# Macaron block on one core: attention runs all heads of batch 0, then all of batch 1

## The chip, the cores and the metric

One core of a Trainium2 chip runs the whole program. Its engines have queues of their own and wait for each other on semaphores: PE (TensorE, matrix multiply), DVE (VectorE), ACT (ScalarE), POOL (GpSimd) and SP (SyncE, which here only issues DMAs). The metric is device microseconds of the slowest core. The kernel before has a median of 596.48 us in three runs (592.13 to 601.65).

## The reference

A macaron block over x of 2 x 512 tokens, 256 wide: half a mixture of experts, attention, half a mixture of experts again, each on a layer-normed x and added to it.

```
x = x + 0.5 * ffn(layernorm(x))
x = x + attention(layernorm(x))
x = x + 0.5 * ffn(layernorm(x))

# attention: B, S, D = 2, 512, 256;  H, HKV, DH = 16, 4, 128;  four query heads share one key/value head
q = rope(x @ wq.T); k = rope(x @ wk.T); v = x @ wv.T
# causal, linear (no softmax); each head h has its own decay lam[h], the same for both batches
o[i] = sum over j <= i of (q[i] . k[j]) * exp(-lam[h] * (i - j)) * v[j]
return o.reshape(b, s, H * DH) @ wo.T
```

The two batches do not meet in attention: what they share are the weights and the decays. The experts' layers (32 experts of 96, 16 small ones of 128, four per token) are not touched.

## The kernel before

The program runs expert layer, attention, expert layer. Attention works in **units**: one head of one batch, 512 tokens. There are 32 (`UNITS`), and unit n is head n // 2 of batch n % 2 (`B` = 2). Four heads share a key/value head, so eight units (`GU`) use one group g; keys and values of group g + 1 are made while group g runs.

Five kinds of work carry a letter in the code. `("q", n, b)` is the query projection of unit n, `("k", g, b)` the key projection, `("v", g, b)` the value projection, `("t", g, b)` the transposition of the first 256 keys, and in the splits `("o", h)` stands for the output weights. `projections(n, place)` says which of them unit n runs: in place "scores" the query projection of unit n + 1, in place "behind" one piece for the next group (v, v, k, k, t, t in units 2 to 7 of a group). The lists `order` and `split_order` are the orders in which all engines go through projections and splits, and positions in them are the values that semaphores wait for.

**Splits.** Query, key and output projections run as three products of high and low parts in place of one. So each weight of 128 x 256 is split in two: ACT copies the high part (`split_hi`, L555) and POOL subtracts it from the whole for the low part (`split_lo`, L448), which raises `w_split`. PE waits for `w_split` before a projection or an output. A split of a query or output weight serves both batches of a head here: 16 + 16, and 4 for keys. `splits(n)` says which splits unit n makes: output weights when n is even, query weights of head (n + 3) // 2 when n is odd, which PE wants in unit n + 2.

**One unit on PE**, in order (L1252 to L1265): scores of the first half (L1193) and the chunk state (L1199), query projection of the next unit (L1180, six matmuls of 512 columns), scores of the second half (L1193), output projection of the unit before (L1231, twelve matmuls), the piece "behind" (L1180, L1171 or L1165), then the products with the values (L1217, L1214).

**Beside it.** DVE subtracts for the low half of the output (L941), applies the decay mask (L932), copies the state (L934), rotates the new query from PSUM (L920 to L922), masks the second half and rotates a key. POOL goes through its unit as follows: add the two parts of the rotated query (L526, raises `roped`, which the next scores wait for), multiply its second half by the decays (L533), make the splits of the unit (L448), add a rotated key if there is one (L526). ACT scales values (L579), makes the high parts (L555), copies projected values and keys (L570), and copies the output from PSUM (L690). All projections but the first five write bank 0 of PSUM, so each waits until the one before it has been read.

**Loads.** SP issues per head: wq after the projection of two heads earlier, decays after `pv_mm`, wo after `wo_mm` (`load_head`, L409), each into one of two buffers, and wk and wv once per group.

**Start and end.** Before unit 0 PE runs q, k, v, v, k, t (`projections(-1, None)`). At the end ACT copies the sums of x and attention out of four PSUM banks (`residual_out`, L672): batch 0's four tiles once output 30 is done, batch 1's after output 31.

## Time and profile before

| | |
|---|---|
| median of three runs | 596.48 us (592.13 to 601.65) |
| profiled execution | 596.83 us, span 595.1 us, mean granted clock 0.929 |
| PE busy | 507.6 us, 85% of the span |
| PE weight load (PEld) busy | 439.8 us, 74% |
| DVE busy | 318.7 us, 54% |
| POOL busy | 257.4 us, 43% |
| ACT busy | 142.8 us, 24% |
| costliest group | L1180, projections from split weights: x240, 65.2 us, 407 ns each |
| chain that ended last | PE 60%, DVE 22%, DMA 11%, issue 3% |

The profile describes one execution. "Busy" leaves out the waits; a line's idle time is what its engine spent before it, with the operation that ended most of it. An average over the span mixes three stages, so what a change in attention is worth must be read from a stretch of attention alone: with start times from the timeline, and busy times from windows.

### The profile page before, as it was taken

Reading aid. Unit: us, or ns where it says so; the run is one execution under the profiler, and the core shown is the slowest. Engines: PE = TensorE matmul, PEld = TensorE weight load, DVE = VectorE, ACT = ScalarE, POOL = GpSimd, SP = SyncE. Lnnn points to the kernel's source line nnn. Section 1 sums busy time; section 2 is a strip of 40 time slices with the busy share of each in tenths; the row PEclk is TensorE's granted clock in tenths of the full one; section 3 lists DMA queues with packets and bytes.
Section 4 is the critical chain, followed back from the end, with each engine's and each line's share of the span. In section 5 each row is a group of like instructions: output and inputs, shape, how many; then the busy total and the mean of one; then the engine's idle time right before and its main releaser. Section 6 shows DMA issues by size and latency. Waiting matters only on the chain.

```text
span 595.1 us, 9863 instructions
## 1 busy us (share of the span) xinstructions
PE 507.6 (85%) x3276; PEld 439.8 (74%) x3276; DVE 318.7 (54%) x997; ACT 142.8 (24%) x382; POOL 257.4 (43%) x280
## 2 busy tenths in 40 slices
PE   8589979999039999999999999999858999999900
PEld 7489968887017888889888988888758898888600
DVE  6844333343296647664766476666785444444325
ACT  4102212222234231222132212211420222222211
POOL 0045656663236444434443444333103566666322
PEclk9789999999559999999999999999976999999955
DMA  7989987781650010121012011110295425778173
GB/s 228 322 261 330 331 319 245 257 287 55 236 192 18 28 36 19 54 56 23 31 40 68 19 36 36 52 37 10 86 381 179 154 94 182 234 251 281 55 256 118
DMA packets 46654, 87.79 MB, mean 148 GB/s; under 512 B 6528, under 2 KB 27264, under 8 KB 46592
## 3 DMA queue, kind: packets, MB, share of 16 engines
q1 hardware_dynamic: 37376, 66.05, 34.0%
q0 software_dynamic: 6912, 18.88, 9.4%
q10 hardware_dynamic: 2304, 2.10, 1.0%
q8 instruction: 31, 0.51, 0.4%
q14 instruction: 31, 0.25, 0.1%
HBM read 74.42 MB, written 12.58 MB: 146 GB/s over the span
## 4 chain that ended last, share of the span: by engine, by line
PE 60%; DVE 22%; DMA 11%; issue 3%; SPq 2%; ACT 1%; POOL 1%; POOLq 0%; DVEq 0%; ACTq 0%
PE bank L1180 10%; PE bank L1089 8%; PE bank L1084 7%; PE bank L1217 6%; DMA w_down_sb<-w_down 4%; PE bank L1108 4%; PE bank L1110 4%; PE bank L1193 4%; DVE shared L921 3%; DVE shared L922 3%; DVE shared L920 3%; DMA shared<-z_dram 3%; PE bank L1214 3%; PE bank L1171 3%; PE bank L1199 2%
## 5 line engine op out<-in xcount | busy, mean ns | idle before, releaser
L458 POOL DMA_INDIRECT decay_all<-xn_dram,ids x72 | 69.6, 966 | 121.0 <-PE bank L1056 52.8
L526 POOL TENSOR_TENSOR shared<-shared 128x512 f32<-128x512 f32 x36 | 45.8, 1273 | 130.2 <-DVE shared L922 130.2
L860 DVE COPY oT_all<-bank 128x256 f32<-128x256 f32 x72 | 30.6, 425 | 131.0 <-PE bank L1056 131.0
L467 POOL DMA_INDIRECT z_dram<-probs_all,dest x72 | 70.2, 975 | 36.4 <-ACT probs_all L642 32.7
L1180 PE MATMUL bank<-split_sb 128*128 128x512 f32 x240 | 65.2, 407 | 1.9 <-ACT split_sb L601 0.9
L1089 PE MATMUL bank<-w_ch_sb,oT_all 128*128 128x256 f32 x256 | 65.7, 379 | 0.0
L941 DVE TENSOR_TENSOR split_sb<-bank,split_sb 128x512 fp32r<-128x512 f32 x32 | 22.1, 692 | 66.2 <-ACT split_sb L690 66.2
L634 ACT ACTIVATE rot<-bank 128x224 f32<-128x224 f32 x72 | 25.7, 357 | 132.2 <-PE bank L1089 132.2
L1084 PE MATMUL bank<-w_exp_sb,oT_all 128*128 128x192 f32 x256 | 53.4, 331 | 2.9 <-issue 1.6
L1231 PE MATMUL bank<-split_sb 128*128 128x256 f32 x384 | 53.4, 288 | 1.5 <-DVE split_sb L941 1.5
L1084 PEld LDWEIGHTS bank<-w_exp_sb,oT_all 128*128 128x128 f32 x256 | 43.8, 189 | 10.3 <-issue 5.5
L1180 PEld LDWEIGHTS bank<-split_sb 128*128 128x128 f32 x240 | 42.2, 189 | 10.7 <-DVE shared L922 1.9
L1089 PEld LDWEIGHTS bank<-w_ch_sb,oT_all 128*128 128x128 f32 x256 | 46.9, 190 | 3.3
L1231 PEld LDWEIGHTS bank<-split_sb 128*128 128x128 f32 x384 | 47.8, 190 | 1.7 <-issue 1.7
L690 ACT ACTIVATE split_sb<-bank 128x512 fp32r<-128x512 f32 x32 | 19.1, 597 | 118.5 <-PE bank L1217 118.5
L642 ACT ACTIVATE probs_all<-bank 128x256 f32<-128x256 f32 x72 | 27.6, 383 | 69.2 <-PE bank L1110 69.2
L920 DVE TENSOR_TENSOR shared<-bank,rot 128x512 f32<-128x512 f32 x40 | 27.7, 691 | 25.7 <-PE bank L1180 25.7
L932 DVE TENSOR_TENSOR probs_all<-bank,decay_all 128x256 f32<-128x256 f32 (+1 forms) x128 | 39.5, 350 | 1.0
L1108 PE MATMUL bank<-w_down_sb,wkv_sb 96*128 96x256 f32 x128 | 38.2, 380 | 0.0
L1110 PE MATMUL bank<-w_ch_sb,wkv_sb 128*128 128x256 f32 x128 | 38.2, 379 | 0.0
L1006 PE MATMUL bank<-ident_sb,xn_sb 128*128 128x128 f32 x48 | 11.3, 325 | 26.2 <-DVE xn_sb L762 25.8
L905 DVE SCALAR_TENSOR_TENSOR x_sb<-shared,wgt,x_sb 128x256 f32<-128x256 f32 x36 | 17.8, 524 | 27.1 <-POOL x_sb L501 27.0
(141 smaller groups left out, 971.3 us busy)
## 6 DMA issues: line engine op xcount, KB each, us to landing
shared<-w_up_piece SPq DMA_DIRECT2D x32, 448.0 KB, 6.3
w_exp_sb<-w_exp SPq DMA_DIRECT2D x32, 384.0 KB, 8.3
shared<-w_down_piece SPq DMA_DIRECT2D x32, 256.0 KB, 4.3
w_ch_sb<-w_ch SPq DMA_DIRECT2D x16, 384.0 KB, 5.9
shared<-z_dram SPq DMA_DIRECT2D x12, 512.0 KB, 7.1
decay_all<-decay SPq DMA_DIRECT2D x16, 256.0 KB, 2.7
w_down_sb<-w_down SPq DMA_DIRECT2D x16, 192.0 KB, 7.8
xn_dram<-xn_sb ACTq DMA_DIRECT2D x16, 128.0 KB, 6.1
```

Source lines behind the costliest of these rows:

```text
L458: pool.indirect_dma_start(out=xg[s], out_offset=None, in_=xn_dram[l][:, :], in_offset=bass.IndirectOffsetOnAxis(ap=ids[:, SEQ[t]:SEQ[t] + ...
L467: pool.indirect_dma_start(out=z_dram[l][:, :], out_offset=bass.IndirectOffsetOnAxis(ap=dest[:, SEQ[t]:SEQ[t] + 1], axis=0), in_=y_sb[s], i ...
L526: nc.gpsimd.tensor_tensor(dst, rope_a[r % 2], rope_b[r % 2], ALU.add).then_inc(roped, 1)
L920: nc.vector.tensor_tensor(rope_a[r % 2], ps[:, :], cos_sb, ALU.mult)
L932: ins = nc.vector.tensor_tensor(probs[c][:, a:b], sc_ps[c][:, a:b], decay_sb[h % 2][:, 0:b - a], ALU.mult)
L1084: nc.tensor.matmul(h2[rows, :, 0:MI], xgT[s][:, k, rows], up_e[:, k * 2 * MI:(k + 1) * 2 * MI].rearrange("p (a n) -> p a n", a=2), start=( ...
L1089: ins = nc.tensor.matmul(h2[rows, :, MI:WI], xgT[s][:, k, rows], up_c[:, k * 2 * CI:(k + 1) * 2 * CI].rearrange("p (a n) -> p a n", a=2), ...
L1108: nc.tensor.matmul(y_ps[s][rows, 0:D], actT[s][0:MI, 0, rows], down_e, start=True, stop=False)
L1110: ins = nc.tensor.matmul(y_ps[s][rows, 0:D], actT[s][:, 1, rows], down_c, start=False, stop=True)
L1180: ins = nc.tensor.matmul(proj_bank[at][:, :], w[:, k, :], x[:, k, b * S:(b + 1) * S], start=(k == 0 and w is hi and x is xnT_hi), stop=(k ...
L1217: ins = nc.tensor.matmul(o_ps[:, j * P:(c + 1) * HALF], v_sb[g % 2][:, b * SB + j, :], probs[c][:, t * HALF:t * HALF + HALF - t * P], star ...
L1231: ins = nc.tensor.matmul(res_ps[(n % B) * SB + t], o[n % 2][:, cols], w, start=False, stop=False, skip_group_check=True)
```

## The change

Unit n becomes head n % 16 of batch n // 16: all heads of batch 0, then all heads of batch 1. A key/value group G now means one group of one batch. It serves four units, there are eight of them (`GS`), and each brings one k, one v and one t, in places m = 1, 2, 3 of the four units of the group before. Key and value buffers are halved accordingly, and no longer lie in `xn_sb`. Since neighbouring units have different heads, every unit loads and splits weights of its own: 32 loads each of wq, wo and decays where there were 16, 8 of wk and wv where there were 4, and 72 splits on ACT and on POOL where there were 36. The split of q is made two units ahead of its unit (`("q", n + 2)` in `splits(n)`), and stands behind that of o. Each unit has its own weights, so the loads are issued piecewise (`load_q`, `load_o`, `load_decay`). Before unit 0 stand q, k, v, t in place of q, k, v, v, k, t, and a third split. The copies of batch 0's four tiles wait for output 15 in place of output 30; their place in ACT's program stays. The indices in ACT's, DVE's and POOL's helpers follow the new units, and are left out of the diff below.

```diff
--- before.py
+++ after.py
@@ -146,11 +146,9 @@
...
         kqT = shared[:, 0:4 * S].rearrange("p (a s) -> p a s", s=S)
         v_all = sb("v_all", [P, TT * DH])
 
-        xn_flat = xn_sb[:, :, :].rearrange("p t d -> p (t d)")
-        kT = [[kqT[:, b, :] for b in range(B)], [xn_flat[:, b * S:(b + 1) * S] for b in range(B)]]
+        kT = [kqT[:, u, :] for u in range(2)]
         qT = [kqT[:, 2 + u, :] for u in range(2)]
-        v_sb = [v_all[:, :].rearrange("p (t d) -> p t d", t=TT),
-                xn_flat[:, B * S:2 * B * S].rearrange("p (t d) -> p t d", t=TT)]
+        v_sb = [v_all[:, u * S:(u + 1) * S].rearrange("p (t d) -> p t d", t=SB) for u in range(2)]
...
@@ -287,35 +284,32 @@
 
 
 
-        UNITS, GU = H * B, GROUPS * B
+        UNITS, GS = H * B, HKV * B
+
 
         def projections(n, place):
 
-
-            g, m = n // GU, n % GU
+            G, m = n // GROUPS, n % GROUPS
             if n < 0:
-                return [("q", 0, 0), ("k", 0, 0), ("v", 0, 0), ("v", 0, 1), ("k", 0, 1), ("t", 0, 0)]
+                return [("q", 0), ("k", 0), ("v", 0), ("t", 0)]
             if place == "scores":
-                return [("q", n + 1, (n + 1) % B)] if n + 1 < UNITS else []
-            if g + 1 < HKV and m >= 2:
-                return [("vvkktt"[m - 2], g + 1, m % 2)]
-            return [("t", 0, 1)] if n == 0 else []
+                return [("q", n + 1)] if n + 1 < UNITS else []
+            return [("vkt"[m - 1], G + 1)] if m >= 1 and G + 1 < GS else []
 
         def splits(n):
 
             if n < 0:
-                return [("q", 0), ("k", 0)]
-            found = [("o", n // 2)] if n % 2 == 0 else [("q", (n + 3) // 2)] if n + 3 < UNITS else []
-            if n == 0:
-                found.append(("q", 1))
-            if n % GU == 3 and n // GU + 1 < HKV:
-                found.append(("k", n // GU + 1))
+                return [("q", 0), ("k", 0), ("q", 1)]
+            found = [("o", n)]
+            if n + 2 < UNITS:
+                found.append(("q", n + 2))
+            if n % GROUPS == 1 and n // GROUPS + 1 < GS:
+                found.append(("k", n // GROUPS + 1))
             return found
 
         def split_buffer(key):
             kind, n = key
             return (kind, 0 if kind == "k" else n % 2)
-
 
         split_order = [key for n in range(-1, UNITS) for key in splits(n)]
         order = projections(-1, None)
@@ -324,7 +318,7 @@
         rotated = [p for p in order if p[0] in "qk"]
         copied = [p for p in order if p[0] in "vt"]
 
-        proj_bank = [bank[a] for a in (2, 3, 6, 0, 1)] + [bank[0]] * (len(order) - 5)
+        proj_bank = [bank[a] for a in (2, 3, 6, 1)] + [bank[0]] * (len(order) - 4)
 
         block = ctx.enter_context(nc.Block())
 
@@ -399,36 +393,50 @@
 
             stage_quads(sp, 0)
 
-            def load_kv(g):
-                if g >= 1:
-
-                    sp.wait_ge(proj_mm, max(order.index((kind, g - 1, 1)) for kind in "kv") + 1)
-                sp.dma_start(wk_sb, wk[g, :, :]).then_inc(kv_in, 16)
-                sp.dma_start(wv_sb, wv[g, :, :]).then_inc(kv_in, 16)
-
-            def load_head(h):
-                u = h % 2
-                if h >= 2:
-                    sp.wait_ge(proj_mm, order.index(("q", 2 * (h - 2) + 1, 1)) + 1)
-                sp.dma_start(wq_sb[u], wq[h, :, :]).then_inc(wq_in[u], 16)
-                if h >= 2:
-                    sp.wait_ge(pv_mm, B * (h - 1))
-                sp.dma_start(decay_sb[u], decay[h, :, :]).then_inc(decay_in[u], 16)
-                if h >= 2:
-                    sp.wait_ge(wo_mm, 2 * (h - 1))
-                sp.dma_start(wo_sb[u], wo[h, :, :]).then_inc(wo_in[u], 16)
+            def load_kv(G):
+                if G >= 1:
+                    sp.wait_ge(proj_mm, max(order.index((kind, G - 1)) for kind in "kv") + 1)
+                sp.dma_start(wk_sb, wk[G % HKV, :, :]).then_inc(kv_in, 16)
+                sp.dma_start(wv_sb, wv[G % HKV, :, :]).then_inc(kv_in, 16)
+
+            def load_q(n):
+                if n >= 2:
+                    sp.wait_ge(proj_mm, order.index(("q", n - 2)) + 1)
+                sp.dma_start(wq_sb[n % 2], wq[n % H, :, :]).then_inc(wq_in[n % 2], 16)
+
+            def load_decay(n):
+                if n >= 2:
+                    sp.wait_ge(masked[1], n - 1)
+                    sp.wait_ge(q_scaled, n - 1)
+                sp.dma_start(decay_sb[n % 2], decay[n % H, :, :]).then_inc(decay_in[n % 2], 16)
+
+            def load_o(n):
+                if n >= 2:
+                    sp.wait_ge(wo_mm, n - 1)
+                sp.dma_start(wo_sb[n % 2], wo[n % H, :, :]).then_inc(wo_in[n % 2], 16)
 
             def first_loads():
                 load_kv(0)
-                load_head(0)
+                load_q(0)
+                load_q(1)
+                load_decay(0)
                 sp.dma_start(cos_sb, cos[:, :]).then_inc(const_in, 16)
                 sp.dma_start(sin_sb, sin[:, :]).then_inc(const_in, 16)
 
             load_results(sp, 0, first_loads)
-            for h in range(1, H):
-                load_head(h)
-                if h % GROUPS == 1 and h // GROUPS + 1 < HKV:
-                    load_kv(h // GROUPS + 1)
+            load_o(0)
+            load_decay(1)
+            load_q(2)
+            load_kv(1)
+            for n in range(UNITS):
+                if n + 3 < UNITS:
+                    load_q(n + 3)
+                if n + 1 < UNITS:
+                    load_o(n + 1)
+                if n + 2 < UNITS:
+                    load_decay(n + 2)
+                if n % GROUPS == 3 and n // GROUPS + 2 < GS:
+                    load_kv(n // GROUPS + 2)
 
             sp.wait_ge(wo_mm, UNITS)
             for c in range(NCH):
@@ -664,13 +671,12 @@
...
         def _(act_e):
             moe_act(act_e, 0)
             norm_act(act_e, 1)
-            copy_projected(act_e, ("v", 0, 0))
+            copy_projected(act_e, ("v", 0))
             scale_values(act_e, 0)
-            copy_projected(act_e, ("v", 0, 1))
-            copy_projected(act_e, ("t", 0, 0))
+            copy_projected(act_e, ("t", 0))
 
             def residual_out(i):
-                act_e.wait_ge(wo_mm, UNITS - 1 if i < SB else UNITS)
+                act_e.wait_ge(wo_mm, H if i < SB else UNITS)
                 nc.scalar.activation(x_sb[:, i, :], res_ps[i], ACT.Copy).then_inc(x2_copied, 1)
...
@@ -1144,25 +1148,22 @@
...
-                kind, n, b = p
+                kind, n = p
+                b = n // H if kind == "q" else n // HKV
                 at = order.index(p)
-                if at == 5:
-                    pe.wait_ge(kv_copied, 2)
+                if at in (3, 4):
+                    pe.wait_ge(xnT_copied, 2 * TT)
                 elif at >= 5 and order[at - 1] in copied:
                     pe.wait_ge(kv_copied, copied.index(order[at - 1]) + 1)
                 elif at >= 5:
                     pe.wait_ge(rope_read, rotated.index(order[at - 1]) + 1)
-                else:
+                if kind != "t":
                     pe.wait_ge(xnT_copied, TT + (b + 1) * SB)
...
@@ -1214,21 +1211,20 @@
...
             def output(n):
-                h = n // B
-                key = ("o", h)
+                key = ("o", n)
                 pe.wait_ge(w_split, split_order.index(key) + 1)
                 pe.wait_ge(o_split, n + 1)
...
                 for t in range(SB):
                     cols = slice(t * P, (t + 1) * P)
                     for o, w in ((oT_hi, hi), (oT_lo, hi), (oT_hi, lo)):
-                        ins = nc.tensor.matmul(res_ps[(n % B) * SB + t], o[n % 2][:, cols], w, start=False, stop=False,
+                        ins = nc.tensor.matmul(res_ps[(n // H) * SB + t], o[n % 2][:, cols], w, start=False, stop=False,
                                                skip_group_check=True)
...
```

The first place is POOL's queue in two neighbouring units early in attention. L526 (L534 after) is the add of the rotated query, L533 (L540) its product with the decays, L448 (L456) a split: wq_all holds query weights, wo_all output weights, wkv_sb key weights. Before:

```order
L526 TENSOR_TENSOR shared<-shared 128x512
L533 TENSOR_TENSOR state_sb<-shared,decay_all 128x256
L448 TENSOR_TENSOR split_sb<-wq_all,split_sb 128x256
L526 TENSOR_TENSOR shared<-shared 128x512
L533 TENSOR_TENSOR state_sb<-shared,decay_all 128x256
L448 TENSOR_TENSOR split_sb<-wo_all,split_sb 128x256
```

After, from the same unit (unit 1, and unit 2):

```order
L534 TENSOR_TENSOR shared<-shared 128x512
L540 TENSOR_TENSOR state_sb<-shared,decay_all 128x256
L456 TENSOR_TENSOR split_sb<-wo_all,split_sb 128x256
L456 TENSOR_TENSOR split_sb<-wq_all,split_sb 128x256
L456 TENSOR_TENSOR split_sb<-wkv_sb,split_sb 128x256
L534 TENSOR_TENSOR shared<-shared 128x512
L540 TENSOR_TENSOR state_sb<-shared,decay_all 128x256
L456 TENSOR_TENSOR split_sb<-wo_all,split_sb 128x256
L456 TENSOR_TENSOR split_sb<-wq_all,split_sb 128x256
```

Each unit now has both splits, o ahead of q, where it had one of the two.

The second place is PE's queue at the start of attention: L1180 (L1181 after) are query and key projections, six rows each, L1171 (L1172) value projections, L1165 (L1166) the transposition, L1193 the first scores. Before:

```order
L1180 MATMUL bank<-split_sb 128x512 x12
L1171 MATMUL bank<-wkv_sb,shared 128x128 x16
L1180 MATMUL bank<-split_sb 128x512 x6
L1165 MATMUL bank<-ident_sb,shared 128x128 x2
L1193 MATMUL bank<-shared 128x256
```

After:

```order
L1181 MATMUL bank<-split_sb 128x512 x12
L1172 MATMUL bank<-wkv_sb,shared 128x128 x8
L1166 MATMUL bank<-ident_sb,shared 128x128 x2
L1193 MATMUL bank<-shared 128x256
L1193 MATMUL bank<-shared 128x128
```

The second value projection and the second key projection are no longer ahead of the first scores.

## Rows read from the trace of the kernel before

**Rows 1.** Windows over attention: stretch, us, busy us by engine, PEclk, DMA share.

```profile
190.80:412.21 221.41, 217.91 (x1342) 193.63 (x1340) 136.10 (x290) 51.61 (x137) 91.56 (x100) 1.00 0.13 38
```

**Rows 2.** Timeline of a plain interval: start us, length us, engine, line, operation.

```profile
392.16 1.64 PE L1180 MATMUL bank<-split_sb 128*128 128x512 f32 x6
...
393.83 0.69 DVE L920 TENSOR_TENSOR shared<-bank,rot 128x512 f32<-128x512 f32 x1 [0.45 <-PE bank L1180]
...
396.00 1.26 POOL L526 TENSOR_TENSOR shared<-shared 128x512 f32<-128x512 f32 x1 [3.93 <-DVE shared L922]
...
397.35 0.73 POOL L533 TENSOR_TENSOR state_sb<-shared,decay_all 128x256 f32<-128x256 f32 x1
...
398.02 0.60 ACT L690 ACTIVATE split_sb<-bank 128x512 fp32r<-128x512 f32 x1 [5.20 <-PE bank L1217]
...
398.03 0.73 POOL L448 TENSOR_TENSOR split_sb<-wq_all,split_sb 128x256 fp32r<-128x256 f32 x1
...
398.84 1.63 PE L1180 MATMUL bank<-split_sb 128*128 128x512 f32 x6
```

**Rows 3.** Timeline, PE: query projections that begin v, k and t intervals.

```profile
213.40 1.63 PE L1180 MATMUL bank<-split_sb 128*128 128x512 f32 x6
...
221.87 1.64 PE L1180 MATMUL bank<-split_sb 128*128 128x512 f32 x6
...
290.13 1.64 PE L1180 MATMUL bank<-split_sb 128*128 128x512 f32 x6
...
298.21 1.64 PE L1180 MATMUL bank<-split_sb 128*128 128x512 f32 x6
...
305.07 1.63 PE L1180 MATMUL bank<-split_sb 128*128 128x512 f32 x6
```

**Rows 4.** Timeline, PE and POOL: the interval with output and query split.

```profile
190.80 1.64 PE L1180 MATMUL bank<-split_sb 128*128 128x512 f32 x6
...
194.71 1.27 POOL L526 TENSOR_TENSOR shared<-shared 128x512 f32<-128x512 f32 x1 [1.58 <-DVE shared L922]
...
196.06 0.72 POOL L533 TENSOR_TENSOR state_sb<-shared,decay_all 128x256 f32<-128x256 f32 x1
...
196.74 0.73 POOL L448 TENSOR_TENSOR split_sb<-wo_all,split_sb 128x256 fp32r<-128x256 f32 x1
...
197.42 0.73 POOL L448 TENSOR_TENSOR split_sb<-wq_all,split_sb 128x256 fp32r<-128x256 f32 x1
...
198.25 1.62 PE L1180 MATMUL bank<-split_sb 128*128 128x512 f32 x6 [0.28 <-issue]
```

**Rows 5.** Timeline, PE and POOL: start of attention.

```profile
180.08 4.23 POOL L508 TENSOR_TENSOR split_sb<-shared,split_sb 128x256 fp32r<-128x256 f32 x6
...
181.68 3.01 PE L1180 MATMUL bank<-split_sb 128*128 128x512 f32 x12 [0.92 <-ACT split_sb L601]
...
184.52 3.73 PE L1171 MATMUL bank<-wkv_sb,shared 128*128 128x128 f32 x32
...
187.71 1.28 POOL L526 TENSOR_TENSOR shared<-shared 128x512 f32<-128x512 f32 x1
...
189.48 0.38 PE L1165 MATMUL bank<-ident_sb,shared 128*128 128x128 f32 x2
```

**Rows 6.** DMA issues with us to landing, and timeline of SP.

```profile
wo_all<-wo SPq DMA_DIRECT2D x5, 128.0 KB, 2.0
...
389.21 0.33 SPq L419 DMA_DIRECT2D wo_all<-wo  x1
```

**Rows 7.** Windows, columns as in the first group, around a low clock.

```profile
148.00:150.00 2.00, 0.34 (x2) 0.00 (x0) 0.00 (x0) 1.07 (x2) 1.52 (x2) 1.00 0.41 133
...
150.00:152.00 2.00, 0.00 (x0) 0.00 (x0) 0.00 (x0) 0.80 (x2) 0.40 (x1) 0.91 0.24 78
...
178.00:180.00 2.00, 1.81 (x8) 0.89 (x8) 1.83 (x9) 2.00 (x9) 1.35 (x2) 0.76 0.00 0
```

**Rows 8.** Timeline, ACT: copy of the last unit's output.

```profile
423.00 0.60 ACT L690 ACTIVATE split_sb<-bank 128x512 fp32r<-128x512 f32 x1 [0.53 <-PE bank L1217]
```

More of the change, by code:

```diff
@@ L557, in copy_projected @@
         def copy_projected(act_e, p):
-            kind, g, b = p
+            kind, G = p
             act_e.wait_ge(proj_mm, order.index(p) + 1)
@@ L941, in split_output @@
                 nc.vector.tensor_tensor(oT_lo[n % 2], o_ps[:, :], oT_hi[n % 2].bitcast(f32), ALU.subtract).then_inc(o_split, 1)
-            rotate(("q", 0, 0))
-            rotate(("k", 0, 0))
-            rotate(("k", 0, 1))
+            rotate(("q", 0))
+            rotate(("k", 0))
             for n in range(UNITS):
@@ L1154, in project @@
                     pe.wait_ge(rope_read, rotated.index(order[at - 1]) + 1)
-                else:
+                if kind != "t":
                     pe.wait_ge(xnT_copied, TT + (b + 1) * SB)
-                if kind == "q":
-                    key = ("q", n // B)
-                elif kind == "k":
-                    key = ("k", n)
                 if kind == "t":
-                    pe.wait_ge(roped, rotated.index(("k", n, b)) + 1)
+                    pe.wait_ge(roped, rotated.index(("k", n)) + 1)
                     for t in range(2):
                         cols = slice(t * P, (t + 1) * P)
-                        ins = nc.tensor.transpose(proj_bank[at][:, cols], kT[n % 2][b][:, cols], ident_sb[:])
+                        ins = nc.tensor.transpose(proj_bank[at][:, cols], kT[n % 2][:, cols], ident_sb[:])
                 elif kind == "v":
@@ L1173, in project @@
                 else:
-                    pe.wait_ge(w_split, split_order.index(key) + 1)
+                    pe.wait_ge(w_split, split_order.index(p) + 1)
                     pe.wait_ge(xnT_split, (b + 1) * SB)
                     hi, lo = [w.rearrange("p (k n) -> p k n", k=KD)
-                              for w in (w_hi[split_buffer(key)], w_lo[split_buffer(key)])]
+                              for w in (w_hi[split_buffer(p)], w_lo[split_buffer(p)])]
                     for k in range(KD):
@@ L1203, in products @@
             def products(n):
-                g, b = n // GU, n % B
+                G = n // GROUPS
                 pe.wait_ge(o_split, n)
-                if n == 0:
-                    pe.wait_ge(rope_read, rotated.index(("k", 0, 1)) + 1)
-                if n % GU < B:
-                    pe.wait_ge(kv_copied, copied.index(("v", g, b)) + 1)
+                pe.wait_ge(kv_copied, copied.index(("v", G)) + 1)
                 for c in range(2):
```

53 lines of the change are left out of this document (25 added, 28 removed).

## The prediction

> **What bounds the kernel now.** I read the page first (PE 85% busy, POOL 43%, ACT 24%), then windows to find attention, then the timeline of all engines in one unit. Attention's main stretch runs from the query projection of unit 1 (190.80) to that of unit 31 (412.21): 221.41 us, with PE busy for 217.91 of them at full clock, and POOL for 91.56 [rows 1]. So on average PE sets the pace and POOL is idle over half the time. That average is not enough here: the change puts work on POOL, and PE waits for POOL's results in a given order.
>
> I therefore measure each unit from one query projection to the next on PE, which I call an interval. A plain one takes 398.84 - 392.16 = 6.68 us [rows 2]. With a value projection behind it takes 221.87 - 213.40 = 8.47, with a key projection 298.21 - 290.13 = 8.08, with a transposition 305.07 - 298.21 = 6.86 [rows 3]. The first, which also holds two residual matmuls and a transposition, takes 198.25 - 190.80 = 7.45 [rows 4]. Before has 30 intervals: 11 plain, 6 of each kind and the first, together 73.5 + 140.5 + 7.45 = 221.4, the whole stretch. So nothing else is in it.
>
> Now POOL inside a plain interval [rows 2]. The query projection starts at 392.16, DVE begins to rotate its result at 393.83, POOL adds it at 396.00 (3.84 after the projection's start), multiplies it by the decays at 397.35 and makes its one split at 398.03, done at 398.76. The next query projection starts at 398.84, but its weights had been split a unit earlier, so it waits for none of this.
>
> **What changes in an interval.** Each unit now makes the output split and then the split of the query weights of two units on, which PE wants in the very next unit. The trace of before shows this pair once, in unit 0, where head 0's output and head 1's query weights are both split: add 194.71, multiply 196.06, split 196.74, split 197.42 to 198.15, and PE starts the projection at 198.25 [rows 4]. This is 3.54 us from the start of the add to the projection that needs its result. All of it hangs on POOL's order: the add cannot begin before the rotation, and the two splits stand behind it, though their inputs have long been there. So the loop is query projection, rotation, add, multiply, split, split, query projection, and it takes 3.84 + 3.54 = 7.38 us. An interval now lasts as long as this or as its old length, whichever is more. A plain one goes from 6.68 to 7.38 (+0.70), one with a transposition from 6.86 to 7.38 (+0.52); those with a value or key projection (8.47, 8.08) hide it, though a key split stands behind the query split in the former, since nobody waits for that one until a unit later.
>
> **How many.** After the change the 30 intervals are: places m = 1, 2, 3 of the first seven groups with v, k and t (7 each), and 9 plain (eight with m = 0, unit 0 among them, and unit 29). Unit 0 keeps its residual matmuls in place of an output projection of about the same length and loses its transposition, so I take it as plain.
> - Without any stall the new mix would take 9 x 6.68 + 7 x (8.47 + 8.08 + 6.86): against before two plain intervals and the first go, and one of each kind comes, -13.36 - 7.45 + 23.41 = **+2.6 us**. This is the value and the key projection that stood before unit 0 and now stand inside.
> - The stall adds 9 x 0.70 + 7 x 0.52 = **+9.9 us**. Its bounds: 0, should POOL's splits be done in time, and 9 x 0.75 + 7 x 0.57 = 10.7, should the splits take their full 0.73 us each in place of the 0.68 between their starts. I take the measured chain.
>
> **The start.** Before unit 0 PE loses eight value and six key matmuls, some 3.5 us of its time. That gives nothing, for the first scores need the rotated key of batch 0, and its way stays: two rotations on DVE, then POOL's add at 187.71, 1.28 long [rows 5]. Before, PE came to the transposition at 189.48, half a microsecond after that add, because of the second projections; now it will wait for the add itself. And a third split on POOL (0.7) now stands before the six subtractions from 180.08, whose second one the first projection (181.68) waits for [rows 5]. So the transposition comes at 187.71 + 0.70 + 1.28 + 0.05 = 189.74, or **+0.3 us**. Bounds: -0.4 if the third split costs nothing, +0.7 if all of it counts.
>
> **What I cost at nothing.** ACT gets 36 more high parts of 0.4 us; it idles 5.20 us ahead of each output copy (row of 398.02 in [rows 2]), and without this cover a unit would take 0.4 more. Loads: SP now issues three per unit. The wo of the next unit goes out when output n - 1 is done, as at 389.21, and lands 2.0 us later [rows 6], at 391.2; ACT comes to its split at about 392.4, once it has copied the output and scaled the values, so 1.2 us are left. Decays go out after the second mask and have over four microseconds. DVE has nothing new. The residual copies of batch 0 (1.2 us) can run earlier, but ACT stands idle 0.53 us just before it copies the last output [rows 8], so they were hidden: 0. The expert layers are as before.
>
> **Sum:** 2.6 + 9.9 + 0.3 = +12.8 us. The profiled execution took 596.83, 0.35 above the median of 596.48; I put the sum on both alike: **609.3 us** as a median, 2.1% slower. The measurement of this kernel tells about 2% from no change, or 608.4 us here.
>
> **Rivals.**
> - *POOL keeps ahead.* The condition is that the query split is done 2.84 us after the add starts, 0.70 earlier than measured in unit 0. Then only the mix and the start count: +2.9, 599.4 us, no change that could be told. For it speaks that POOL is idle more than half of the stretch, against it that its idle time lies before the add. The Trainium skill (GPSIMD Engine Reference, section 3.1) gives about 2.6 cycles per element for an operation with two inputs, at 1.2 GHz; by that a split is an estimated 0.56 us and the add 1.11, the chain would take some 2.8 us in place of 3.54, and this rival would hold. The rows stand against it: 0.73 for a split or a product and 1.27 for the add [rows 2, 4].
> - *The clock falls in the gap at the start.* With less before unit 0, PE idles from about 187.2 (the one value projection then ends) to 189.7, 2.5 us. After PE's last work of the first expert layer the clock stayed full for over 1.6 us beyond 150, where PE had done only 0.34 us in the 2 us before, and later was back only within 178 to 180 (0.76 there) [rows 7]. A fall would cost about 2 to 4 us of matmuls at half speed: near 612. The Trainium skill (TensorE: Matmul & The Clock Gate, Part 1) calls the half clock the default that only activity releases; it would allow such a fall, and the trace has none for so short a gap.
> - *A load comes late.* Should wo take over 3.2 us, ACT's split of o and with it q's would slip. It needs nearly 4 us, twice what is measured, before POOL waits too. Each microsecond of that in 30 units would be 30 us: 620 or more.
> - *Faster.* Everything taken away, 3.5 us of PE at the start and 1.2 us on ACT, stays under 12 us even if it all counted.
>
> **Numbers.** Forecast 0.81, its own range 606 to 613 with the scatter of medians (the three runs lie 0.8% to either side). POOL keeps ahead 0.09, clock 0.05, late load 0.03, something faster 0.02. The range 602 to 615 leaves out the first rival's centre and the late load. Slower by over 2% means above 608.4: three in five of the forecast (0.49), and the clock and load rivals (0.08) give 0.57; faster 0.02; within 2% 0.41.
>
> **What would show it.** In the profile after, plain intervals of 7.38 us with POOL's second split ending just before each query projection on PE, and PE idle there, released by POOL's split line; value and key intervals unchanged at 8.47 and 8.08; the transposition at about 189.7 behind POOL's add, counted from the same start; attention's stretch near 234 us. Plain intervals of 6.68 would prove the first rival, longer ones with ACT waiting for a DMA the third, a PEclk of 0.5 near 190 the second. If value or key intervals grow too, the loop is longer than I measured.

## The result, and the profile after

The changed kernel took **612.78 us** (median of four runs, 611.56 to 617.05) beside 596.32 for the kernel before (592.13 to 601.65): ratio **1.0313, 95% interval 1.023 to 1.0396**. The ratios and intervals here and below are taken over fast executions alone, so they are not the quotients of the medians. The forecast was 609.3, slower, with a range of 602 to 615. Sign and range were right; the median is 3.5 us above the forecast.

The profiled execution of the changed kernel took 611.56 us (span 609.9). First the page: busy time per engine, the chain that ended last, and the group of the query projection.

```profile
PE 515.9 (85%) x3276; PEld 444.3 (73%) x3276; DVE 320.4 (53%) x997; ACT 153.6 (25%) x418; POOL 282.5 (46%) x316
...
PE 33%; issue 22%; POOL 21%; DVE 10%; DMA 10%; SPq 2%; ACT 1%; POOLq 0%; DVEq 0%; ACTq 0%
...
L1181 PE MATMUL bank<-split_sb 128*128 128x512 f32 x240 | 65.0, 407 | 10.0 <-POOL split_sb L456 8.8
```

PE is still busy for 85% of the span, and a reader of the first line alone would call it the bound as before. The second line says otherwise: of the chain that ended last, PE holds 33% where it held 60%, and POOL 21%. The third says where: the query projection (L1180 before, L1181 now) idles 10.0 us, 8.8 of them behind POOL's split. The list of waits over attention (us in total, times, longest) counts them:

```profile
PEld bank L1181 <- issue: 11.4, 16, 0.8
PE bank L1181 <- POOL split_sb L456: 8.8, 16, 0.6
...
PE bank L1166 <- POOL shared L534: 2.7, 1, 2.7
```

Sixteen waits: nine plain intervals and seven with a transposition, the number that the prediction gave. Here is PE in four successive intervals, one of each kind (k, t, plain, v), from the timeline:

```profile
273.33 1.63 PE L1181 MATMUL bank<-split_sb 128*128 128x512 f32 x6
...
281.41 1.62 PE L1181 MATMUL bank<-split_sb 128*128 128x512 f32 x6
...
288.98 1.63 PE L1181 MATMUL bank<-split_sb 128*128 128x512 f32 x6 [0.48 <-POOL split_sb L456]
...
296.52 1.62 PE L1181 MATMUL bank<-split_sb 128*128 128x512 f32 x6 [0.62 <-POOL split_sb L456]
...
304.98 0.71 PE L1181 MATMUL bank<-split_sb 128*128 128x512 f32 x2
```

The value interval is 304.98 - 296.52 = 8.46 and the key interval 281.41 - 273.33 = 8.08, as before [rows 3]. The transposition's went from 6.86 to 288.98 - 281.41 = 7.57, the plain one from 6.68 [rows 2] to 296.52 - 288.98 = 7.54. The windows over attention, in the columns of [rows 1]; the second is from the first projection to unit 1's:

```profile
194.02:430.50 236.48, 224.49 (x1363) 197.84 (x1362) 138.10 (x293) 63.06 (x173) 114.99 (x134) 1.00 0.26 74
185.22:194.02 8.80, 6.14 (x38) 5.41 (x39) 4.14 (x6) 2.68 (x9) 5.91 (x7) 1.00 0.14 45
```

So the stretch from unit 1's query projection to unit 31's grew from 221.41 to 236.48, **+15.07 us**; PE's work in it grew by 224.49 - 217.91 = 6.6, with 12.0 us of idle time in place of 3.5. One whole loop, in the timeline of PE and POOL:

```profile
320.59 1.62 PE L1181 MATMUL bank<-split_sb 128*128 128x512 f32 x6 [0.44 <-POOL split_sb L456]
...
324.43 1.27 POOL L534 TENSOR_TENSOR shared<-shared 128x512 f32<-128x512 f32 x1 [4.09 <-DVE shared L928]
...
325.77 0.73 POOL L540 TENSOR_TENSOR state_sb<-shared,decay_all 128x256 f32<-128x256 f32 x1
...
326.46 0.73 POOL L456 TENSOR_TENSOR split_sb<-wo_all,split_sb 128x256 fp32r<-128x256 f32 x1
...
327.15 0.73 POOL L456 TENSOR_TENSOR split_sb<-wq_all,split_sb 128x256 fp32r<-128x256 f32 x1
...
328.10 0.53 PEld L1181 LDWEIGHTS bank<-split_sb 128*128 128x128 f32 x3 [0.78 <-issue]
328.13 0.70 PE L1181 MATMUL bank<-split_sb 128*128 128x512 f32 x2 [0.62 <-POOL split_sb L456]
```

This is the shape of [rows 4], now in the middle of attention. Projection to addition takes 324.43 - 320.59 = 3.84, as predicted. Addition to next projection takes 328.13 - 324.43 = 3.70 in place of 3.54. The split ends at 327.15 + 0.73 = 327.88 and PE starts 0.25 later; in [rows 4] it started 198.25 - (197.42 + 0.73) = 0.10 later.

For the start, both kernels are counted from their first row transposition of the attention part, since up to there PE's program is the same: 167.66 before, 170.52 after. That these lie 2.86 apart is scatter, for the kernels below, equal up to this point, have it between 164.77 and 168.40. Part of it can be seen: in the first expert layer the clock of the changed kernel's profile falls once more, behind a PE gap of 3.08 us (0.53 over 82 to 84 us, 0.62 over 84 to 86), where the kernel before has 1.00 behind a gap of 3.58 us.

```profile
167.66 0.69 PE L1006 MATMUL bank<-ident_sb,xn_sb 128*128 128x128 f32 x2 [19.32 <-DVE xn_sb L762]
```
```profile
170.52 0.69 PE L1010 MATMUL bank<-ident_sb,xn_sb 128*128 128x128 f32 x2 [19.82 <-DVE xn_sb L768]
...
185.22 3.01 PE L1181 MATMUL bank<-split_sb 128*128 128x512 f32 x12 [0.45 <-ACT split_sb L608]
...
192.67 0.41 PE L1166 MATMUL bank<-ident_sb,shared 128*128 128x128 f32 x2 [2.65 <-POOL shared L534]
...
194.02 1.17 PE L1181 MATMUL bank<-split_sb 128*128 128x512 f32 x4
```

From there the first projection comes after 14.70 us (before 14.02, [rows 5]), the transposition after 22.15 (before 21.82), unit 1's projection after 23.50 (before 23.14, [rows 4]): the start costs +0.36.

The two profiled times differ by 611.56 - 596.83 = 14.73: +2.86 before attention, +0.36 at the start, +15.07 in the stretch, -3.56 behind unit 31's projection. Of the last, nothing lies in attention, for output 31 follows that projection by about 12.25 us in both; all of it lies in the second expert layer, which is the same code. The first and the last number together are -0.7 and scatter; attention is what has to be explained.

### The profile page after: what moved, and what is told of

Read it like the earlier page. It is cut to its first block, busy times and chain, and to the rows that moved or that the text cites. A ratio compares the mean times of both kernels' runs of the same rounds, so it can differ in the third digit from the quotient of the medians.

```text
span 609.9 us, 10064 instructions
## 1 busy us (share of the span) xinstructions
PE 515.9 (85%) x3276; PEld 444.3 (73%) x3276; DVE 320.4 (53%) x997; ACT 153.6 (25%) x418; POOL 282.5 (46%) x316
## 4 chain that ended last, share of the span: by engine, by line
PE 33%; issue 22%; POOL 21%; DVE 10%; DMA 10%; SPq 2%; ACT 1%; POOLq 0%; DVEq 0%; ACTq 0%
PE bank L1093 8%; POOL shared L534 8%; POOL split_sb L456 8%; PE bank L1088 7%; DMA w_down_sb<-w_down 4%; PE bank L1112 4%; PE bank L1114 4%; POOL state_sb L540 4%; DVE x_sb L911 3%; PE bank L1060 2%; PE bank L1001 2%; DMA shared<-w_up_piece 2%; DMA shared<-z_dram 1%; PE bank L1102 1%; DMA probs_all<-z_dram 1%
## 5 line engine op out<-in xcount | busy, mean ns | idle before, releaser
L534 POOL TENSOR_TENSOR shared<-shared 128x512 f32<-128x512 f32 x40 | 51.0, 1276 | 125.8 <-DVE shared L928 125.7
L1181 PE MATMUL bank<-split_sb 128*128 128x512 f32 x240 | 65.0, 407 | 10.0 <-POOL split_sb L456 8.8
L1181 PEld LDWEIGHTS bank<-split_sb 128*128 128x128 f32 x240 | 42.1, 188 | 21.3 <-issue 11.4
L1193 PE MATMUL bank<-shared 128*128 128x256 f32 (+1 forms) x256 | 52.3, 327 | 0.0
L1214 PE MATMUL bank<-probs_all,v_all 128*128 128x256 f32 (+1 forms) x256 | 52.2, 326 | 0.0
L1214 PEld LDWEIGHTS bank<-probs_all,v_all 128*128 128x128 f32 x256 | 46.8, 190 | 6.1 <-issue 0.5
L1193 PEld LDWEIGHTS bank<-shared 128*128 128x128 f32 x256 | 46.0, 190 | 5.9
```

The source lines that it names most:

```text
L534: nc.gpsimd.tensor_tensor(dst, rope_a[r % 2], rope_b[r % 2], ALU.add).then_inc(roped, 1)
L1181: ins = nc.tensor.matmul(proj_bank[at][:, :], w[:, k, :], x[:, k, b * S:(b + 1) * S], start=(k == 0 and w is hi and x is xnT_hi), stop=(k ...
L1193: ins = nc.tensor.matmul(sc_ps[c][:, t * HALF:t * HALF + HALF - t * P], kT[G % 2][:, j * P:(j + 1) * P], qT[n % 2][:, j * P:(c + 1) * HALF ...
L1214: ins = nc.tensor.matmul(o_ps[:, j * P:(c + 1) * HALF], v_sb[G % 2][:, j, :], probs[c][:, t * HALF:t * HALF + HALF - t * P], start=(j == 0 ...
```

## Experiments

Theory A: attention loses its time because POOL ends the query split too late for the next projection (the loop above), plus what PE adds before it starts. The rivals: the amount of POOL's work, the order of batches itself (more work or other waits inside the stretch), the clock. Each kernel below is compared with the kernel before, run on the same chip (median 595.22 for kernels 1 to 4, 596.57 for 5 to 8, 595.54 for 9). The recorded expectations use labels: e1 to e4 are kernels 1 to 4, e7 is kernel 5, e5 kernel 6, e6 kernel 7, e9 kernel 8 and e8 kernel 9; q1 and q31 are the query projections of units 1 and 31.

**1. Query split ahead of the output split.** The changed kernel, with the two splits of a unit swapped.

```diff
-            found = [("o", n)]
-            if n + 2 < UNITS:
-                found.append(("q", n + 2))
+            found = [("q", n + 2)] if n + 2 < UNITS else []
+            found.append(("o", n))
```

> The changed kernel, with the query split ahead of the output split in each unit, on ACT and POOL. Same work, same number of splits. Theory (PE waits for a chain on POOL: add, multiply, split o, split q): the chain gets one split shorter, 7.54 - 0.68 = 6.86 us, so plain intervals take 6.86 and those with a transposition stay at their old 6.86; 9 x 0.68 + 7 x 0.68 = 10.9 us less than after: near 602, stretch from q1 to q31 near 225.6. Rival (POOL has too much to do in all, or the added loads and high parts cost the time): no change, 612.8.

Measured: **602.64 us** (600.81 to 603.79), ratio 1.0124 [1.0091, 1.0156]. Plain intervals and those with a transposition are both 6.85. One plain interval in the timeline of PE and POOL:

```profile
313.24 1.63 PE L1180 MATMUL bank<-split_sb 128*128 128x512 f32 x6
...
317.08 1.26 POOL L533 TENSOR_TENSOR shared<-shared 128x512 f32<-128x512 f32 x1 [3.41 <-DVE shared L927]
...
319.11 0.73 POOL L455 TENSOR_TENSOR split_sb<-wq_all,split_sb 128x256 fp32r<-128x256 f32 x1
...
320.09 0.70 PE L1180 MATMUL bank<-split_sb 128*128 128x512 f32 x2
```

One split of 0.68 has left the loop, and the plain interval fell by 7.54 - 6.85 = 0.69. POOL does as much as before and the batches have the same order. In plain intervals the loop still decides: the addition comes 3.84 after the projection, the split ends at 319.84, and PE starts 0.25 later. In those with a transposition it no longer does: 6.85 is PE's own length there, as in kernel 2 below. The stretch is 226.31, 0.7 above the 225.6 expected: the first interval is 7.69, for the clock fell there, as in kernel 2.

**2. POOL's splits ahead of its addition.** The changed kernel; POOL makes the splits while it would wait for DVE's rotation.

```diff
             for n in range(-1, UNITS):
+                if n >= 0:
+                    for key in splits(n):
+                        split_lo(pool, key)
                 for p in projections(n, "scores"):
                     if p in rotated:
                         add_rotated(p)
                 if n >= 0:
-                    for key in splits(n):
-                        split_lo(pool, key)
```

> The changed kernel, with POOL's splits of a unit ahead of its add of the rotated query, where POOL stands idle. Same work. Theory: the query split is done some 3 us before PE wants it, no interval waits for POOL, plain 6.68 and transposition 6.86 us; 9 x 0.86 + 7 x 0.68 = 12.5 us less than after, near 600.3, stretch q1 to q31 near 224.0. What is left over before is the new mix of intervals (2.6) and the start. Rival (amount of work): 612.8.

Measured: **600.48 us** (595.21 to 603.66), ratio 1.0076 [1.0038, 1.0114]. Plain intervals are 6.68 again, with transposition 6.85, value 8.46, key 8.08; the stretch is 224.64. So 11.8 of the changed kernel's 15.07 us are gone with one move on POOL. But the first interval is 7.40, where no wait explains it. PE there, from the timeline, and the windows around it (the clock is the third number from the end):

```profile
189.67 0.41 PE L1167 MATMUL bank<-ident_sb,shared 128*128 128x128 f32 x2 [2.66 <-POOL shared L534]
189.92 1.42 PE L1194 MATMUL bank<-shared 128*128 128x256 f32 x4
...
191.84 2.35 PE L1182 MATMUL bank<-split_sb 128*128 128x512 f32 x6
```
```profile
188.00:190.00 2.00, 0.33 (x3) 0.36 (x4) 0.18 (x1) 0.37 (x2) 1.47 (x2) 1.00 0.46 131
190.00:192.00 2.00, 2.00 (x10) 1.82 (x9) 0.00 (x0) 1.57 (x5) 0.54 (x1) 0.50 0.00 0
192.00:194.00 2.00, 2.00 (x7) 1.60 (x7) 0.82 (x3) 0.00 (x0) 0.88 (x2) 0.65 0.00 0
```

After PE's 2.66 us of idleness behind POOL's addition the granted clock falls to 0.50, which is 1.2 GHz: four score matmuls take 1.42 in place of 0.82, six of the projection 2.35 in place of 1.62. From transposition to unit 2's projection it costs 2.17 + 7.40 in place of 1.35 + 6.68, **1.5 us**. In the profile of the changed kernel the clock stayed at 1.00 behind the same gap (2.65).

**3. The same, with 45 us more work on POOL.** Kernel 2, with two more subtractions of 128 x 256 in each unit, whose results nobody reads.

```diff
+                if 0 <= n < UNITS - 1:
+                    for u in range(2):
+                        nc.gpsimd.tensor_tensor(state_sb[:, (8 + u) * D:(9 + u) * D], w_ch_sb[:, 0:D],
+                                                w_ch_sb[:, D:2 * D], ALU.subtract)
```

> As e2_splits_before_add, with two further subtractions of 128 x 256 on POOL in each of 31 units, behind the splits and ahead of the add; their results go nowhere. That is 62 x 0.73 = 45 us more of POOL's time. Theory (place counts, not amount): splits and subtractions end some 3.6 us after the query projection starts, the add is due at 3.84, so no more than 1 us over e2, where a key split stands there too. Rival (POOL's amount of work sets the pace): 30 us or more over e2.

Measured: **598.06 us** (597.19 to 601.48), ratio 1.0071 [1.0036, 1.0105]. The window over its stretch, and POOL in one unit:

```profile
191.61:415.53 223.92, 220.72 (x1363) 196.63 (x1362) 137.20 (x291) 62.43 (x172) 157.88 (x194) 1.00 0.27 78
```
```profile
313.37 0.73 POOL L456 TENSOR_TENSOR split_sb<-wq_all,split_sb 128x256 fp32r<-128x256 f32 x1
314.06 1.44 POOL L548 TENSOR_TENSOR state_sb<-w_ch_sb 128x256 f32<-128x256 f32 x2
315.78 1.26 POOL L534 TENSOR_TENSOR shared<-shared 128x512 f32<-128x512 f32 x1 [0.28 <-DVE shared L933]
```

POOL is busy for 157.88 us of the stretch (114.99 in the changed kernel, whose stretch is 12.6 us longer), yet in most units it still waits 0.16 to 0.28 for DVE before the addition. Where a key split stands there too, the addition comes late (202.49 - 198.29 = 4.20 after the projection in place of 3.84), and the interval, one with a value projection, is 8.47 all the same. The rival "amount of work" falls: 43 us more cost nothing, since they stand where POOL waited. Its clock stayed full, and 223.92 is the stretch without a stall: 2.5 above the 221.41 of before, for which the prediction's change of mix had +2.6.

**4. Fewer waits ahead of a projection.** The changed kernel; its query projection has three further waits behind the one on the split. Two of them are long satisfied and left out here, so that one is left.

```diff
-                if kind != "t":
+                if kind != "t" and at < 3:
                     pe.wait_ge(xnT_copied, TT + (b + 1) * SB)
...
                     pe.wait_ge(w_split, split_order.index(p) + 1)
-                    pe.wait_ge(xnT_split, (b + 1) * SB)
+                    if at < 2 or p == ("k", HKV):
+                        pe.wait_ge(xnT_split, (b + 1) * SB)
```

> The changed kernel without two of the waits ahead of each query projection on PE, those for the transposed input and for its split parts, which have held since the start (kept where they are new). Theory A: PE takes 0.22 us from the end of POOL's split to its weight load in place of the 0.07 seen before because three further waits stand behind the one for the split: with one left, some 0.15 us less in each of the 16 waiting intervals, 7.39 in place of 7.54, 610.4 in all. Theory B: the 0.22 belongs to the hand-over from POOL itself: 7.54 stays, 612.8.

Measured: **610.95 us** (609.22 to 612.53), ratio 1.0276 [1.0248, 1.0304]. In the timeline:

```profile
321.71 0.73 POOL L456 TENSOR_TENSOR split_sb<-wq_all,split_sb 128x256 fp32r<-128x256 f32 x1
...
322.58 1.16 PE L1182 MATMUL bank<-split_sb 128*128 128x512 f32 x4 [0.50 <-POOL split_sb L456]
```

The split ends at 322.44 and PE starts 0.14 later, in place of 0.25; intervals are 7.41 to 7.44 in place of 7.54, and the stretch 234.84, 1.64 shorter, although the clock fell at its start here too. The times can't show this term, for the interval of the changed kernel (1.023 to 1.0396) contains that of this one; the trace does.

What PE's queue waits for ahead of such a projection can be read from the records of its waiting instructions (the kernel before in unit 0, then two of the changed kernel):

```profile
L1175 PEldq EVENT_SEMAPHORE  x1: 2032/2032/2032, 196.2 to 196.2; - x1
```
```profile
L1175 PEldq EVENT_SEMAPHORE  x1: 51/51/51, 327.9 to 327.9; - x1
```
```profile
L1176 PEldq EVENT_SEMAPHORE  x1: 51/51/51, 328.0 to 328.0; - x1
```

Before, one instruction waited 2.03 us for POOL's split and for the input's split parts together, and the weight load behind it had one wait of its own. In the changed kernel the first instruction waits for the split alone; a second one, 0.11 us later, waits for the input's split parts and for the transposed input (the wait that the diff gives to every projection), and the weight load comes behind it, again with one of its own. So three waits stand behind that on the split where there was one, in another order than the source lists them. Kernel 4 has the first of these two instructions and the weight load, and not the second.

**5. Before, with late splits.** The other way round: the kernel before, with no work added and batches alternating, but each head's query weights split one unit later, beside the output's.

```diff
-            found = [("o", n // 2)] if n % 2 == 0 else [("q", (n + 3) // 2)] if n + 3 < UNITS else []
-            if n == 0:
-                found.append(("q", 1))
+            found = [("o", n // 2)] if n % 2 == 0 else []
+            if n % 2 == 0 and n + 2 < UNITS:
+                found.append(("q", (n + 2) // 2))
```

> The kernel before, batches alternating, one split per weight and head as ever (36 in all), but the query weights of a head are split one unit later, in the even unit just ahead of their first projection, behind the output weights. No work is added. Theory (lateness, not amount or batch order): each even interval of plain or transposition length now waits for POOL's add, multiply, split o, split q: five plain and three with a transposition, 0.70 to 0.86 and 0.52 to 0.68 each, 5 to 6.3 us over before, near 601 to 602. Rival (amount of splits, or the loads): no change, 595.5.

Measured: **602.69 us** (598.52 to 607.6), ratio 1.0087 [1.0049, 1.0126].

```profile
251.11 1.64 PE L1180 MATMUL bank<-split_sb 128*128 128x512 f32 x6
...
257.67 0.73 POOL L448 TENSOR_TENSOR split_sb<-wq_all,split_sb 128x256 fp32r<-128x256 f32 x1
...
258.50 0.70 PE L1180 MATMUL bank<-split_sb 128*128 128x512 f32 x2 [0.46 <-issue]
```

PE's idle time there is put down to "issue"; that the split ends it is read from the times. The interval is 258.50 - 251.11 = 7.39, to 0.01 the loop that the prediction had worked out, and PE starts 0.10 after the split. Five plain intervals at +0.71 and three with a transposition at +0.53 are 5.1; the stretch grew by 226.37 - 221.41 = 4.96, the ratio says 5.2 us. So the stall comes from when the split is made, with the old order of batches as with the new.

**6. Unit 1's low part behind the six subtractions.** Kernel 2; at the start POOL makes this split after the subtractions that PE waits for.

```diff
-                    for key in splits(-1):
+                    for key in splits(-1)[:2]:
                         split_lo(pool, key)
...
+            if l == 0:
+                split_lo(pool, splits(-1)[2])
```

> As e2_splits_before_add, with the low part of unit 1's query weights made on POOL behind the six subtractions at the start instead of ahead of them. Theory: this split is what shifted the start; the first query projection starts 0.7 us sooner after the last row transposition, and with it rotation, add and the transposition of keys. Read from the profile: first projection to transposition stays at 7.45 us (as 192.67 - 185.22 in the changed kernel), last row transposition (PE) to first projection 0.7 less than the 1.39 there. Rival: the projection waits for ACT's copies, and nothing moves.

Measured: 597.34 us in a single execution, too little to compare times; its trace:

```profile
166.62 0.69 PE L1013 MATMUL bank<-ident_sb,xn_sb 128*128 128x128 f32 x2 [19.15 <-DVE xn_sb L771]
...
180.64 3.01 PE L1184 MATMUL bank<-split_sb 128*128 128x512 f32 x12 [0.24 <-ACT split_sb L611]
...
188.08 0.41 PE L1169 MATMUL bank<-ident_sb,shared 128*128 128x128 f32 x2 [2.64 <-POOL shared L536]
189.43 2.89 PE L1184 MATMUL bank<-split_sb 128*128 128x512 f32 x6
```

First row transposition to first projection is 14.02 again, the value of before, where all kernels with three splits at this place have 14.69 to 14.71. So the third split costs its full 0.68 there, and the rival (ACT's copies) falls. The clock fell here as well (0.50 from 190 to 192; six projection matmuls took 2.89).

**7. Unit 1's query projection in the gap.** Kernel 6; the projection moves from behind the transposition to before it, where PE idled. DVE rotates its result at the start too, and the first projections use one bank more; these lines are left out below.

```diff
-                return [("q", 0), ("k", 0), ("v", 0), ("t", 0)]
+                return [("q", 0), ("k", 0), ("v", 0), ("q", 1), ("t", 0)]
...
-                return [("q", n + 1)] if n + 1 < UNITS else []
+                return [("q", n + 1)] if 1 <= n < UNITS - 1 else []
```

> As e5_q1_split_late, with the query projection of unit 1 moved ahead of the transposition, into the gap in which PE waits for the rotated key. Theory: PE has 1.6 us of work in a gap of 2.65, the first interval gets that much shorter (transposition to the query projection of unit 2: 8.0 in e3, near 6.5 here), and PEclk stays 1.00 near 190 where it fell to 0.50 in e1, e2 and e4 and cost some 1.5 us there. 1.5 to 3 us less than e2: 597 to 599 in all. Rival: the rotation of that query delays the first masks on DVE by as much, and the time stays.

Measured: **595.62 us** (593.61 to 598.3), ratio 0.9975 [0.9939, 1.0012].

```profile
185.17 1.62 PE L1185 MATMUL bank<-split_sb 128*128 128x512 f32 x6
...
188.05 0.41 PE L1170 MATMUL bank<-ident_sb,shared 128*128 128x128 f32 x2 [1.27 <-POOL shared L536]
...
194.62 1.64 PE L1185 MATMUL bank<-split_sb 128*128 128x512 f32 x6
```

The time is below the 597 to 599 that was expected. The gap is 1.27 in place of 2.64, the clock is 1.00 in every window from 182 to 190, and the transposition is followed by unit 2's projection after 194.62 - 188.05 = 6.57 (8.03 in kernel 3). From the first projection to unit 31's, this kernel takes 411.87 - 180.62 = 231.25 us, before 230.53 and the changed kernel 245.28. All the heads of one batch and then the other, and with these three moves no loss that the interval (0.6% down to 0.1% up) could tell: the order of batches itself costs next to nothing.

**8. The gap filled with idle matmuls.** Kernel 2, with twelve matmuls on ones, whose results nobody reads, ahead of the first transposition.

```diff
                     for p in projections(-1, None):
+                        if p[0] == "t":
+                            keep_busy(12)
                         project(p)
```

> As e2_splits_before_add, with 12 matmuls of 128 x 128 on ones ahead of the key transposition at the start, whose result nobody reads: about 2 us of PE's time in a gap of 2.65. Theory: the clock fell in e1, e2 and e4 because PE stood idle there; with fillers PEclk stays 1.00 at the first scores, the span from first projection to q1 is 8.8 us as in e3 and the first interval 6.68 in place of 7.40. Up to 1.5 us less than e2. Rival: the clock falls for another reason and does so here too.

Measured: 600.02 us (595.17 to 602.37), ratio 1.0042 [1.0009, 1.0075]; of the ten executions one took 1337.51; its cause is open, and the ratio and the range given here leave it out. The profile has two records for each of the twelve matmuls:

```profile
186.89 2.84 PE L1002 MATMUL bank<-idle_ones 128*128 128x128 f32 x24
189.70 0.41 PE L1167 MATMUL bank<-ident_sb,shared 128*128 128x128 f32 x2
```
```profile
188.00:190.00 2.00, 2.00 (x19) 1.87 (x18) 0.21 (x1) 0.42 (x2) 1.51 (x2) 1.00 0.42 131
190.00:192.00 2.00, 2.00 (x14) 1.81 (x13) 0.57 (x3) 1.58 (x5) 0.50 (x1) 1.00 0.00 0
```

The trace shows what was meant: no gap, clock 1.00 from 188 to 192, first interval 6.68, stretch 223.86. That kernel 2's clock fell because of the gap fits this, but it is not shown: with the gap the clock stayed full in two profiles of six, so one profile without a gap could be chance, and so, less likely, could the three of kernels 7, 8 and 9. The times can't confirm it either: 1.0042 against 1.0076, with intervals that overlap.

**9. Kernel 7 with the shorter list of waits.** The two waits of kernel 4 are left out again.

```diff
-                if kind != "t":
+                if kind != "t" and at < 3:
...
-                    pe.wait_ge(xnT_split, (b + 1) * SB)
+                    if at < 2 or p == ("k", HKV):
+                        pe.wait_ge(xnT_split, (b + 1) * SB)
```

> The run with unit 1's query projection in the gap (heads of batch 0 first, POOL's splits ahead of its addition, the low part of unit 1's queries split late), now with the shorter list of waits on the projections as well. Theory A (a satisfied wait costs 0.06 us only where it stands behind the one that releases a late projection): the query projections don't wait for POOL here, so there is nothing to shorten; intervals stay 6.68 plain, 6.85 with the fourth transposition, 8.46 and 8.08 beside projections; 594 to 597 us, within 1% of the kernel before. Theory B (each wait in the list costs PE its time, released late or not): 32 projections by 0.12 us, 3.8 us less, 592 us.

Measured: **596.72 us** (594.01 to 600.65), ratio 1.0015 [0.9978, 1.0052]. The stretch from unit 2's projection to unit 31's is 413.69 - 196.43 = 217.26 (217.25 in kernel 7). Waits that are all satisfied in time cost nothing here; the rival of this run, 3.8 us less, falls. Neither 7 nor 9 beats the kernel before; both equal it within 0.6%.

## Why the prediction was right

- **Interval under POOL's loop: right in kind and number, short in size.** All sixteen waits are where it said, value and key intervals did not move. Kernels 1 and 2 remove the loop piece by piece and the plain intervals follow (7.54, 6.85, 6.68); kernel 3 shows that POOL's amount of work does not matter, and kernel 5 creates the loop without the change.
- **The mis-sized term** is the stall: +9.9 predicted, 236.48 - 223.92 = +12.6 measured (changed kernel less kernel 3). Within it, it is the last link, POOL's second split to PE's start: 0.10 in [rows 4], 0.25 in the changed kernel. From addition to next projection this makes 3.70 in place of 3.54, and 16 x 0.16 = 2.6 us, the whole difference between the +12.5 predicted for the stretch and the +15.07 measured. In the kernel before one wait stands behind that on the split, in the changed one three (kernel 4 shows PE's queue). Kernel 4 takes two of them away, in one instruction, and gets 0.11 back; the last 0.04 stay open. The prediction took the hand-over from a row with another list of waits, and the diff showed that the list differs.
- **Mix:** +2.6 predicted, +2.5 in kernels 3 (223.92) and 8 (223.86), where nothing stalls.
- **Start:** +0.3 predicted, +0.36 measured (+0.33 at the transposition). The third split counts in full (0.68), and it is partly paid back because PE no longer comes to the transposition late.
- **Costed at nothing:** ACT's added high parts, the loads of wo and the other queues appear among no waits of PE within the stretch. The residual copies of batch 0 run early, and before the last output's copy ACT now idles 2.92 us where it idled 0.53 [rows 8], but output 31 did not come sooner.
- **Rival "POOL keeps ahead": false here.** Addition and split take 1.27 and 0.73 in the changed kernel too. By an estimate from the cycles per element of the Trainium skill (GPSIMD Engine Reference, section 3.1) it would have been true; the rows of before spoke against it, and so does the trace. The rival is true of kernel 2, by the splits' place and not by their length.
- **Rival "clock": given too little chance.** The changed kernel's own profile doesn't show it (1.00 from 190 on), but five other kernels have the same gap of 2.64 to 2.66 us, and in four of them (1, 2, 4, 6) the clock fell to 0.50; kernel 3's stayed full. The price was lower than the 2 to 4 us forecast: 1.5. Whether some of the changed kernel's other runs (median 1.2 above the profiled one) had it is open. The prediction read [rows 7] as saying that so short a gap is safe. The Trainium skill (TensorE: Matmul & The Clock Gate, Part 1) calls the half clock the default that activity releases, and these four traces agree with it. The two without a fall show that a gap of this length need not bring one.
- **The rest of the miss.** Of the 3.5 us in the median, 2.6 are explained. What is left is within the scatter: PE's program, the same up to the first row transposition, reached it between 164.77 and 170.52. The ratio puts the whole loss at 3.1%, some 18.6 us, where the trace shows 15.4 in attention (start and stretch); the interval reaches down to 2.3%, 13.7 us, so these 3 us may be scatter, and no run here shows more.

## What to carry to other kernels

Averages hid this one: POOL had half the stretch idle and 43 us more work cost it nothing, yet two splits of 0.7 us in the wrong place cost over 12, because they stood behind an addition that itself waits for DVE, and PE needed the second of them at once. When a change makes a producer deliver just in time, write out the loop from consumer back to consumer, with its hand-overs taken from rows with the same list of waits, and compare it with the length of each kind of iteration. On such an engine, order the work with ready inputs ahead of the work that has to wait.

## What the runs showed of the hardware

- From the end of POOL's operation to the start of the PE instruction that waited for it: 0.10 and 0.14 us with one further satisfied wait behind (kernels 5 and 4), 0.25 with three (the changed kernel and 1). The two waits more sat in one instruction of the queue; whether each wait costs some 0.06 or the instruction costs 0.11, no run here separates. Waits that were all satisfied when PE came cost nothing that shows (kernel 9).
- A PE gap of 2.64 to 2.66 us, behind a busy stretch at full clock, was followed by a clock of 0.50 in four of six profiles, and by no fall in two, with nearly the same instructions around it. In kernel 2 the fall took 1.5 us.
- POOL's operations took 0.72 to 0.74 us for 128 x 256 and 1.26 to 1.30 for 128 x 512, and those of 128 x 256 started 0.68 to 0.69 apart: half the elements took more than half the time.
